# Pad rows of the experts: eight plain transfers from SP's queue in place of eight indirect ones on GpSimd

## The reference, cut to what matters

```
x = x + attention(layernorm(x), ctx)
xf = layernorm(x)
topk_p, topk_i = top_k(softmax(xf @ router_w.T), 2)      # normalised over the two
for e in range(8):
    mask   = (topk_i == e).any(-1)
    mean_w = sum(topk_p * (topk_i == e)) / sum(mask)
    h      = silu(xf @ gate_w[e].T) * (xf @ up_w[e].T)
    out   += mask * (h @ down_w[e].T) * mean_w
x = x + out
```

## Time and profile before

| | |
|---|---|
| Median of 3 runs | 530.24 us (530.02 to 531.54) |
| Span of the profiled execution | 528.9 us |
| What lies around the span, median less span | 1.3 us |
| PE busy | 476.4 us (90%) |
| DVE, ACT, POOL busy | 321.5, 265.6, 186.4 us |
| Mean granted TensorE clock | 0.954 of full speed |

### The profile page before, as it was taken

One profiled execution on the slowest core, in us unless ns is written; L12 is line 12 of the kernel. 1 busy time (PEld: TensorE's weight loads), 2 busy tenths in 40 slices (PEclk: granted clock), 3 DMA queues, 4 the chain that ended last, 5 costly groups with the idle time before them and its releaser, 6 DMA issues. The chain is left out here.

```text
span 528.9 us, 10721 instructions
## 1 busy us (share of the span) xinstructions
PE 476.4 (90%) x2879; PEld 375.3 (71%) x2880; DVE 321.5 (61%) x827; ACT 265.6 (50%) x878; POOL 186.4 (35%) x211
## 2 busy tenths in 40 slices
PE   2999999999999983199999999999999999999980
PEld 2656666665666542078888888888888888888870
DVE  3476988989998656345665456655655555553430
ACT  1287777677777870044544445544444444532320
POOL 5201327355372434712332323323333232232232
PEclk9699999999999995579999999999999999999996
DMA  7166102112020171371531634415317212112110
GB/s 210 33 184 241 32 12 54 32 34 63 7 58 14 50 286 47 96 274 32 168 117 35 215 83 139 147 32 196 101 20 256 42 20 32 27 21 39 20 20 10
DMA packets 21738, 46.26 MB, mean 87 GB/s; under 512 B 5032, under 2 KB 18600, under 8 KB 20684
## 3 DMA queue, kind: packets, MB, share of 16 engines
q10 hardware_dynamic: 1982, 23.29, 11.6%
q1 hardware_dynamic: 12974, 14.34, 9.3%
q0 software_dynamic: 6752, 8.29, 9.2%
HBM read 34.21 MB, written 10.04 MB: 84 GB/s over the span
## 5 line engine op out<-in xcount | busy, mean ns | idle before, releaser
L752 ACT ACTIVATE probs<-b_s,negmax 100x100 f32<-100x100 f32 x256 | 85.6, 358 | 25.2 <-DVE negmax L1005 21.8
L615 PE MATMUL b_s<-w_hi,x_hi 128*128 128x512 f32 x180 | 77.1, 428 | 1.1 <-issue 1.1
L617 PE MATMUL b_s<-w_hi,x_lo 128*128 128x512 f32 x180 | 72.3, 402 | 0.0
L616 PE MATMUL b_s<-w_lo,x_hi 128*128 128x512 f32 x180 | 72.2, 401 | 0.0
L640 PE MATMUL b_pv<-w_hi,h_hi 128*128 128x256 f32 x240 | 69.8, 291 | 1.4 <-DVE h_lo L1102 1.4
L640 PE MATMUL b_pv<-w_hi,h_lo 128*128 128x256 f32 x240 | 67.4, 281 | 0.0
L640 PE MATMUL b_pv<-w_lo,h_hi 128*128 128x256 f32 x240 | 67.3, 280 | 0.0
L1245 POOL TENSOR_SCALAR y_sb<-y_raw,mean 128x256 f32<-128x256 f32 x30 | 32.8, 1093 | 75.9 <-DVE y_raw L1109 75.7
L1250 POOL DMA_INDIRECT out<-y_sb,idnow x30 | 49.1, 1638 | 25.6 <-issue 23.0
L780 ACT CAST h_hi<-b_small 128x512 fp32r<-128x512 f32 x30 | 17.6, 587 | 80.7 <-PE b_small L631 80.7
L1116 DVE TENSOR_TENSOR w_lo<-w_raw,w_hi x84 | 57.3, 682 | 0.0
(11 more groups left out here) (142 smaller groups left out, 1004.1 us busy)
## 6 DMA issues: line engine op xcount, KB each, us to landing
w_raw<-in_ffw ACTq DMA_DIRECT2D x7, 3072.0 KB, 10.1
xin<-slots SPq DMA_DIRECT2D x30, 128.5 KB
w_raw<-in_ffw SPq DMA_DIRECT2D x1, 3072.0 KB, 10.8
kblk<-krot SPq DMA_DIRECT2D x128, 12.5 KB, 1.8
out<-x_all SPq DMA_DIRECT2D x8, 200.0 KB
ctx_all<-in_ctxT SPq DMA_DIRECT2D x1, 1200.0 KB, 6.1
x_all<-in_x SPq DMA_DIRECT2D x1, 1200.0 KB
cst<-in_consts SPq DMA_DIRECT2D x1, 539.0 KB, 7.5
```

Source lines behind the costliest of these rows:

```text
L615: pe.matmul(o, lh, rh, start=(k == 0), stop=False)
L616: pe.matmul(o, lh, rl, start=False, stop=False)
L617: m = pe.matmul(o, ll, rh, start=False, stop=(k == n - 1))
L752: m = nc.scalar.activation(probs[:, N % 3, h, :], b_s[N % 3][0:S, h * S:(h + 1) * S], ACT.Exp, bias=negmax[:, N % 4, h:h + 1], accum_out=p ...
```

## The change

The eight indirect transfers on POOL go. SP writes each expert's pad rows by one plain transfer of 128 contiguous rows, whose start is e x REGION + count, with the count read from the new tile `counts` (1 x 8, int32) into a register. VectorE writes `counts` where it wrote `taili`. The fill of the last column of `tailrow` moves on POOL from behind all scatters to the first pair. SP waits for both (s_tailrow, s_counts) and issues the eight transfers behind its last store and ahead of the wait for s_first and the scatters. The constant table loses eight of its 1078 columns.

```
-            V.tensor_tensor(taili[:, :], cnt[:, :], cst[:, C_TAIL:C_TAIL + E], ALU.add).then_inc(s_tail, 1)
+            V.tensor_copy(counts[:, :], cnt[0:1, :]).then_inc(s_counts, 1)

@@ sync, behind store_x2(NPAIR - 1)
+            sp.wait_ge(s_tailrow, 1)
+            sp.wait_ge(s_counts, 1)
+            for e in range(E):
+                count = sp.value_load(counts[0:1, e:e + 1], min_val=0, max_val=TOK)
+                end = nc.s_assert_within(e * REGION + count, 0, E * REGION - TILE)
+                sp.dma_start(slots[bass.ds(end, TILE), :], tailrow[:, :]).then_inc(s_tails[e], 16)
             sp.wait_ge(s_first, 1)

@@ gpsimd, in the loop over pairs
+                if i == 0:
+                    g.wait_ge(s_pad, 16)
+                    G.tensor_copy(tailrow[:, D:RW].bitcast(I32), rows_sb[:, B:B + 1]).then_inc(s_tailrow, 1)
@@ gpsimd, behind the loop
-            g.wait_ge(s_pad, 16)
-            G.tensor_copy(tailrow[:, D:RW].bitcast(I32), rows_sb[:, B:B + 1]).then_inc(pool_self, 1)
-            ps[0] += 1
-            g.wait_ge(pool_self, ps[0])
-            g.wait_ge(s_tail, 1)
-            for e in range(E):
-                G.indirect_dma_start(slots, bass.IndirectOffsetOnAxis(taili[:, e:e + 1], 0),
-                                     tailrow[:, :], None).then_inc(s_tails[e], 16)
```

More of the change, by code:

```diff
@@ L61 @@
 C_BASE = C_EXP + E
-C_TAIL = C_BASE + E
-C_THR = C_TAIL + E
+C_THR = C_BASE + E
 C_LT = C_THR + E * (MAXT - 1)
@@ L88, in shape_constants @@
     c[:, C_BASE:C_BASE + E] = np.arange(E) * REGION
-    c[:, C_TAIL:C_TAIL + E] = np.arange(E) * REGION + p[:, None]
     c[:, C_THR:C_LT] = np.tile(TILE * np.arange(1, MAXT), E)
@@ L168, in build @@
         meanw = sb("meanw", [P, E])
-        taili = sb("taili", [P, E], U32)
+        counts = sb("counts", [1, E], I32)
         tailrow = sb("tailrow", [P, RW])
@@ L310, in build @@
         s_scaled = sem("s_scaled")
-        s_tail = sem("s_tail")
+        s_tailrow = sem("s_tailrow")
+        s_counts = sem("s_counts")
         s_tails = [sem(f"s_tails{e}") for e in range(E)]
```

## The result

The changed kernel takes 533.25 us (median of 4 runs, 532.75 to 533.59) against 530.33 for the kernel before on the same chip: ratio 1.0041, 95% interval 1.0023 to 1.0059. It is 2.9 us slower by the medians and 2.2 (1.2 to 3.1) by the ratio; forecast were 2.6 and 532.8 us. The profiled execution spans 531.6 us, 2.7 more than before.

The account below looks back on a forecast made before the run. PE bounds the second stage, and SP's tile load starts it. Eight pad groups on SP, 8.8 us less 6.6 hidden, cost 2.2, plus 0.4 for slow issues: +2.6 on 530.24, 532.8 us; range 530.2 to 536.2.

Parts of the forecast that it names:

- What starts the second stage: Start of second stage: SP's tile load into xin, held by the scatters' wait, starts PE; any delay moves the end equally.
- The eight groups: SP ahead of the scatters' wait: eight pad groups of 1.10 us make 8.8, 6.6 hidden, so 2.2 us paid.
- The 0.4 us allowed for a slow issue: SP's nine microseconds of issuing: allowance for slow issues, one of which costs 1.0 us; 0.4 us, a choice.
- The chain behind: From SP passing the scatters' wait to PE's first transpose: 4.9 us, kept unchanged from the kernel before.
- these are paid once per run, the first pad group pays them: SP's slow first executions: if paid by the first pad group instead of the tile load, the sum stands.
- its faster rival: SP's pad groups cheap at 0.77 us, tile load's slow steps due to POOL's pad issues: 1.7 us faster, 528.5; chance 0.08.
- the point of decision: Length of one pad group on SP, 0.82 us: above it the delay eats the faster rival's gain.
- 2.2 and 0.4: PE's start: 2.2 us later from SP's pad groups, plus 0.4 us allowed for slow issues.
- The Trainium skill's floor: SP's register loads: about 600 ns each by the page, 2.6 us beyond the sum, 535.4 us; the trace's 276 ns was preferred.
- The Trainium skill's rule that simple stores go to the sync engine: Pad transfers on SP: path called generally faster, speaking for the faster side; plain issue 0.33 us, indirect 0.97 to 1.01 on POOL.
- The clock: PE's clock rise at the start of the second stage: taken as zero, 1.4 us either way as bound.
- The end: POOL's last DRAIN of 5.79 us: taken as zero, with 0.7 us saved as a bound if it grows with indirect transfers.

Follow-up runs that it names:

- e3: The changed kernel with each of the eight counts read into a register twice, transfers the same: 536.71 us, ratio 1.0119 to the kernel before.
- e4: The changed kernel with a second transfer of 128 pad rows behind each of the eight: 537.22 us, ratio 1.0121 to the kernel before.
- e8: e5 with eight indirect transfers of pad rows added on POOL behind the last scatter: 530.27 us, ratio 0.9992 to the kernel before.
- e7: The kernel before with eight more indirect transfers of pad rows on POOL, to rows nothing reads: 541.59 us, ratio 1.0202.
- e1: The changed kernel with the eight pad groups moved from SP's queue to ACT's: 530.84 us, ratio 1.0001 to the kernel before.
- e2: The changed kernel with the pad groups of experts 4 to 7 moved behind expert 0's tile loads: 530.28 us, ratio 0.9992 to the kernel before.
- e5: The changed kernel with only expert 0's pads ahead of the scatters' wait, others behind tile loads, expert 0's tile numbers read ahead: 528.46 us, ratio 0.9946 to before.
- e6: The kernel before, pads on POOL, with only expert 0's tile numbers read ahead of the scatters' wait: ratio 0.9999 to the kernel before.

## Why the prediction was right

**What starts the second stage** was read rightly: the tile load on SP, and with it PE 1:1. e3 and e4 move both.

**The eight groups** were sized at 1.10 us. The last four are exactly that (216.83 to 221.2, 4.4 us). The first four took 1.25 to 1.47 us, since loads were slow beside the scatters and one step took 0.6 us more. In all 9.8 us in place of 8.8, with 0.3 more to the semaphore: SP is past it at 221.5, not 220.2. The 0.4 us allowed for a slow issue was too little for this, and most of the excess, 0.75 of 1.1 us in the first four groups, lay in the register loads, for which nothing was allowed.

**The chain behind** was taken over whole, 4.9 us; it measured 4.2. The step that failed is "these are paid once per run, the first pad group pays them". The gap ahead of the transfer was not the cost of a first execution: it belonged to POOL's pad transfers, as e8 shows, and went with them. For the slow first load this is not shown: it takes 635 and 626 ns with POOL's pad transfers (before, e7), but still 479 and 433 without them (e1, after), and 272 to 274 only in e2 and e3. The prediction had POOL as the mechanism of its faster rival, and for the gap it was true; the group length of 1.10 us, above the 0.82 us given as the point of decision, still put the result on the slow side. The two errors, +1.3 and -0.7, leave +2.8 at PE's start where 2.2 and 0.4 were forecast. That the second error makes good half of the first is luck.

**The Trainium skill's floor** for a tensor_load, about 600 ns ("DMA: Bandwidth & Descriptors", "Latency and other measured facts"), was set against the rows, and the rows decided rightly: 0.26 to 0.49 us in all eight. The Trainium skill's rule that simple stores go to the sync engine ("DMA: Bandwidth & Descriptors", section "Issuing engine by pattern") agrees with e5, at a ratio of 0.9946, where the plain path does not stand ahead of the tile load, and not with the changed kernel, at 1.0041, where it does.

**The clock** moved by little: it rose 5.2 us after the first wide matmul in place of 6.0, and the first output of the experts (y_raw) was 2.76 us late where the transpose was 2.83.

**The end.** The DRAIN was priced at zero with 0.7 as a bound. It was the bound: 5.79, 5.14 and 6.45 us with 70, 62 and 78 indirect transfers, 83 ns each, three times on a line. That is a term of the sum mis-sized by 0.66 us. It did not show in the span, because the second stage was 0.6 us longer: from the first to the last copy of row numbers

```profile
L1092 DVE COPY idnext<-xin x30: 143/144/145, 224.5 to 504.9; 128x1 int32 x29, 128x1 int32<-128x1 int32 x1
```
```profile
L1097 DVE COPY idnext<-xin x30: 142/144/144, 227.3 to 508.3; 128x1 int32 x29, 128x1 int32<-128x1 int32 x1
```

it takes 280.4 us before and 281.0 after. This is no doing of the change as far as the profiles tell: e2, whose second stage differs only by four pad groups on SP, has 279.6 and e5, the fastest kernel, 280.3, and a tile's period is 9.53 to 9.56 us between them without a pattern in the edits. What sets it is open.

So the sum for the profile is +3.56 (SP past the semaphore) - 0.73 (chain) + 0.53 (period) - 0.66 (DRAIN) = +2.70, the measured difference of the spans. That the last two terms, both taken as zero, cancel is luck again. The path and the price of a quiet group were right on their merits; the range of 530.2 to 536.2 was wide enough to hold "no change" as well.

## What to carry to other kernels

Moving transfers to a "faster" queue moves their serial issue too: count what then stands ahead of the critical instruction of that queue, here 8 x 1.1 us against 6.6 us of cover. Seven of the eight groups behind the tile loads, with expert 0's tile numbers read ahead of the wait (e5), turned +0.4% into -0.5%; reading them ahead alone gained nothing (e6). Long unbroken runs of indirect transfers on GpSimd should not lie where other engines must branch or issue; their price there does not stand on POOL's own rows.

## What the runs showed of the hardware that was not expected

- While POOL issued indirect transfers back to back for ten microseconds and more, register steps of SP, ACT and DVE, normally under 0.1 us, took up to 0.7 us each. With 16 in a row the run took 10.6 us more (e7), a part of it through the lower clock that followed and 0.65 through the DRAIN.
- POOL's last DRAIN takes 83 ns for every indirect transfer of the run.
- Plain pad transfers beside indirect scatters delay the scatters' landing. By the landings in the trace the last scatter is in 2.7 us after its issue with one pad group or none ahead (before, e5, e6, e7), 3.4 with eight at 1.1 to 1.5 us from each other (after), 5.3 with sixteen transfers (e4), and 2.7 again with the groups 1.7 to 1.9 us apart at that place (e3). That points at how close they stand; no run varies this alone. In e1 the tile load, issued beside pad transfers from ACT's queue, took 2.6 us to the first transpose in place of 2.2.
